# Replacing a score-maximum pass by a norm bound, and a DMA half-swap by a permutation matmul, in an attention and mixture-of-experts kernel

## The reference

```python
# x: (8, 2048, 1024); 8 heads of 128
x = x + attn(layernorm(x))
x = x + ffn(layernorm(x))

def attn(x):
    q, k, v = x @ w_aq, x @ w_ak, x @ w_av      # per head, 128 wide
    q, k = rope(q), rope(k)
    # rope: even, odd = split(x, 2)  (the two halves of the 128)
    #       concat([even*cos - odd*sin, even*sin + odd*cos])
    s = q @ k.T / 128 - 1e30 * (i < j)
    return (softmax(s) @ v) @ w_ao

def ffn(x):   # 8 experts, top 2, and a shared expert of the same size
    cw = softmax(top2(x @ router_w.T)), scattered to 8 columns
    y  = sum_e cw[:, e] * ((silu(x @ w1[e]) * (x @ w3[e])) @ w2[e])
    return y + (silu(x @ sw1) * (x @ sw3)) @ sw2
```

## Time and profile before

| | us |
|---|---|
| two runs | 5095.28 and 5520.56 (median 5307.92) |
| the profiled execution, its own time | 5095.1 |
| its span on the slowest core, number 6 | 5093.6 |
| spans of the eight cores | 5062.8 to 5093.6 |
| TensorE matmul busy | 4199.3 (82%) |
| vector engine busy | 1829.2 (36%) |
| scalar engine busy | 578.0 (11%) |
| Q and K of head 0 start | 266.1 |
| last output slice of head 7 done | 1647.6 |

### The profile page before, as it was taken

The page is one execution under the profiler, slowest core; times in us unless marked ns, Lnnn a source line. Parts: engine busy times, 40 slices in busy tenths (PEclk is TensorE's granted clock), DMA queues, the critical chain, the costliest instruction groups (busy, mean ns, idle before and its releaser), DMA issues.

```text
span 5093.6 us, 49716 instructions; the slowest of 8 cores (5062.8 to 5093.6 us)
## 1 busy us (share of the span) xinstructions
PE 4199.3 (82%) x16850; PEld 1700.1 (33%) x16850; DVE 1829.2 (36%) x3012; ACT 578.0 (11%) x917; POOL 358.7 (7%) x393
## 2 busy tenths in 40 slices
PE   5355557555656549999999999999999999999998
PEld 2111112111111214444444444444444444444443
DVE  4654454455444543223223232232232222322323
ACT  0002111201222001001011011010010110110100
POOL 0000000000000001101011011011010010110100
PEclk9666667766676769999999999999999899999997
DMA  4010000000000124434344434444344334344422
GB/s 94 0 22 8 13 13 0 13 13 13 1 10 2 13 21 38 38 34 40 36 38 38 38 34 38 37 38 38 34 38 37 32 35 38 34 38 39 41 28 77
DMA packets 490854, 151.46 MB, mean 30 GB/s; under 512 B 475642, under 2 KB 486250, under 8 KB 490610
## 3 DMA queue, kind: packets, MB, share of 16 engines
q0 software_dynamic: 475488, 122.72, 26.5%
q1 hardware_dynamic: 15122, 25.56, 1.6%
HBM read 254.12 MB, written 8.39 MB: 52 GB/s over the span
## 4 chain that ended last, share of the span: by engine, by line
PE 74%; DVE 16%; issue 4%; DMA 4%; ACT 1%; DVEq 1%; SPq 1%; ACTq 0%
PE ps L844 20%; PE ps L857 20%; PE ps L905 20%; DVE m_all L513 4%; DMA s_sb<-s_sb 3%; DVE s_sb L590 2%; PE ps L555 2%; PE ps L560 2%; PE ps L569 2%; PE ps L594 1%; ACT pT L581 1%; PE ps L640 1%; PE ps L442 1%; DVE ps L575 1%; DVE s_sb L475 1%
## 5 line engine op out<-in xcount | busy, mean ns | idle before, releaser
L844 PE MATMUL ps<-xn_sb,w_sb 128*128 128x512 bf16 x4608 | 1074.8, 387 | 3.8 <-DVE s_sb L827 3.8
L857 PE MATMUL ps<-xn_sb,w_sb 128*128 128x512 bf16 x4608 | 1056.1, 383 | 0.0
L905 PE MATMUL ps<-big,w_sb 128*128 128x512 bf16 x4608 | 1007.6, 382 | 25.5 <-DVE big L878 25.5
L873 DVE TENSOR_TENSOR s_sb<-ps,s_sb 128x512 bf16<-128x512 f32 x512 | 354.2, 692 | 1205.4 <-PE ps L857 1178.7
L844 PEld LDWEIGHTS ps<-xn_sb,w_sb 128*128 128x128 bf16 x4608 | 457.6, 99 | 583.3 <-issue 87.1
L905 PEld LDWEIGHTS ps<-big,w_sb 128*128 128x128 bf16 x4608 | 453.7, 98 | 579.4 <-issue 45.0
L864 ACT ACTIVATE s_sb<-ps 128x512 bf16<-128x512 f32 x576 | 343.9, 597 | 2663.6 <-PE ps L844 2632.3
L857 PEld LDWEIGHTS ps<-xn_sb,w_sb 128*128 128x128 bf16 x4608 | 454.3, 99 | 554.5 <-issue 46.7
L208 POOL DMA_DIRECT2D w_sb<-w x360 | 333.9, 932 | 2961.7 <-PE ps L857 1828.3
L913 DVE TENSOR_TENSOR x_sb<-x_sb,ps 128x512 f32<-128x512 f32 x288 | 197.9, 687 | 835.5 <-PE ps L905 811.9
L581 ACT ACTIVATE pT<-ps,negmh 128x512 bf16<-128x512 f32 x320 | 219.8, 687 | 1201.0 <-DVE ps L575 932.4
(11 more groups left out here) (105 smaller groups left out, 1339.7 us busy)
## 6 DMA issues: line engine op xcount, KB each, us to landing
w_sb<-w POOLq DMA_DIRECT2D x288, 256.0 KB, 6.3
w_sb<-w POOLq DMA_DIRECT2D x72, 512.0 KB, 8.7
big<-x SPq DMA_DIRECT2D x4, 2048.0 KB, 14.7
s_sb<-s_sb SPq DMA_DIRECT2D x128, 64.0 KB, 2.0
out<-big SPq DMA_DIRECT2D x4, 2048.0 KB, 6.8
w_sb<-wv POOLq DMA_DIRECT2D x2, 1024.0 KB, 20.8
w_sb<-wq POOLq DMA_DIRECT2D x8, 256.0 KB, 5.5
w_sb<-wk POOLq DMA_DIRECT2D x8, 256.0 KB, 6.6
```

The source lines that it names most:

```text
L844: e.matmul(o, l, r, start=s0, stop=s1),
L857: e.matmul(o, l, r, start=s0, stop=s1),
L873: e.tensor_mul(o, i, c),
L905: e.matmul(o, l, r, start=s0, stop=s1),
```

## The change

Two things are rewritten in the attention stage, and nothing else.

First, the half-swap of the rotation. Q (and then K) is now made in all four slices first, 32 matmuls in a row into `ps0` to `ps3`. After them come four steps, one for each slice: cast to bf16, a matmul by a constant 128x128 matrix of 0, 1 and -1 that swaps and signs the halves (into `ps4` or `ps5`), the product with the cosines, the product of the swapped bank with the sines, and the sum. The two DMAs of each slice are gone.

Second, the constant of the head. Instead of the largest score, a bound on it is used: the largest squared norm of a query times the largest squared norm of a key, root taken by Ln and Exp, times 1.02. The squares are made by the vector engine into `pT`, a buffer for each of Q and K, summed over the partitions by a one-column matmul, and reduced on one partition. `emit_mh` is gone; its spreading matmul now ends `emit_passA`, ahead of the next head's Q and K. The matrix is one more 32 KB constant that is loaded at the start.

```diff
+    P = np.zeros((128, 128), dtype=np.float32)
+    for rr in range(64):
+        P[rr, rr + 64] = -1.0
+        P[rr + 64, rr] = 1.0
+    pmat = np.ascontiguousarray(P.T).astype(ml_dtypes.bfloat16)
...
+    t_pmat = dma(ld, "sync", pmat_sb[:, :], d["c_pmat"])
...
             for ts in range(NTS):
-                sl = ts % 2
-                bank = ps[which * 2 + sl]
+                bank = ps[ts]
                 for kc in range(KC):
...
+            for ts in range(NTS):
+                sl = ts % 2
+                bank = ps[ts]
+                pqb = ps[4 + sl]
                 te = bank_cons(bank, "vector",
                                lambda e, o=qb, i=bank.ap[:, :]: e.tensor_copy(o, i),
-                               waits=[qb_swap_tok[sl]])
+                               waits=[qb_free_tok[sl]])
+                qb_free_tok[sl] = bank_prod(pqb,
+                                            lambda e, o=pqb.ap[:, :], r=qb:
+                                            e.matmul(o, pmat_sb[:, :], r,
+                                                     start=True, stop=True),
+                                            waits=[te, t_pmat])
...
-                dma(sw_rope4[sl], "sync", qsw[0:64, :], qb[64:128, :],
-                    waits=[te, sw_last_t2[sl]])
-                d2 = dma(sw_rope4[sl], "sync", qsw[64:128, :], qb[0:64, :])
-                t2 = b.emit("vector",
-                            lambda e, o=rope_t1[1], i=qsw, c=tsn: e.tensor_mul(o, i, c),
-                            waits=[t_sn, d2], incs=[(dv, 1)])[0]
+                bank_cons(pqb, "vector",
+                          lambda e, o=rope_t1[1], i=pqb.ap[:, :], c=tsn:
+                          e.tensor_mul(o, i, c),
+                          waits=[t_sn])
...
     def emit_passA(h):
-        for qi in range(NTT):
-            for ck in range(qi // 4 + 1):
-                bank = ps[4 + ck % 2]
-                bank_prod(bank,
-                          lambda e, o=bank.ap[:, :],
-                          l=qs[:, qi * 128:(qi + 1) * 128],
-                          r=ks[:, ck * 512:(ck + 1) * 512]:
-                          e.matmul(o, l, r, start=True, stop=True),
-                          waits=[rope_done[h]])
-                bank_cons(bank, "vector",
-                          lambda e, i=bank.ap[:, :], o=m_all[:, ci:ci + 1]:
-                          e.reduce_max(o, i, axis=AX.X))
+        sq_scr = [pT[:, 0:512], pT[:, 512:1024]]
+        for which in range(2):
+            src = qs if which == 0 else ks
+            t_prev_mm = pT_free[0]
+            for ts in range(NTS):
+                tsq = b.emit("vector",
+                             lambda e, o=sq_scr[which],
+                             i=src[:, ts * 512:(ts + 1) * 512]: e.tensor_mul(o, i, i),
+                             waits=[rope_done[h], t_prev_mm], incs=[(dv, 1)])[0]
+                t_prev_mm = bank_prod(bank,
+                                      lambda e, o=bank.ap[0:1, :], r=sq_scr[which],
+                                      s0=(ts == 0), s1=(ts == NTS - 1):
+                                      e.matmul(o, onesb[:, :], r, start=s0, stop=s1),
+                                      waits=[tsq], last=True)
+            bank_cons(bank, "vector",
+                      lambda e, o=mh_row[0:1, which:which + 1], i=bank.ap[0:1, :]:
+                      e.reduce_max(o, i, axis=AX.X))
...
     for h in range(NH):
-        t_macc = emit_passA(h)
+        t_negmh = emit_passA(h)
...
-        t_negmh = emit_mh(h, t_macc)
```

More of the change, by code:

```diff
@@ L107, in host_consts @@
     return {"c_cs": cs_full, "c_sn": sn_signed, "c_mask": maskM,
-            "c_identb": identb, "c_identf": identf}
+            "c_identb": identb, "c_identf": identf, "c_pmat": pmat}
 def build_nc(dbg=False):
@@ L129, in build_nc @@
     d["c_identf"] = nc.dram_tensor("c_identf", [128, 128], F32, kind="ExternalInput").ap()
+    d["c_pmat"] = nc.dram_tensor("c_pmat", [128, 128], BF16, kind="ExternalInput").ap()
     d["out"] = nc.dram_tensor("out", [T, DM], F32, kind="ExternalOutput").ap()
@@ L152, in build_nc @@
     identf = nc.alloc_sbuf_tensor("identf", [128, 128], F32)
+    pmat_sb = nc.alloc_sbuf_tensor("pmat_sb", [128, 128], BF16)
     onesb = nc.alloc_sbuf_tensor("onesb", [128, 1], BF16)
@@ L174, in build_nc @@
     negmh = nc.alloc_sbuf_tensor("negmh", [128, 1], F32)
+    mh_sb = nc.alloc_sbuf_tensor("mh_sb", [1, 8], F32)
     bigf = big[:, :].bitcast(F32)
@@ L235, in build_nc @@
     t_constsg = (ldg, ldg.n)
-    t_identb = t_identf = t_mask = t_eb = t_consts
+    t_identb = t_identf = t_mask = t_eb = t_pmat = t_consts
     t_rw = t_cs = t_sn = t_constsg
@@ L421, in build_nc @@
     rope_qb = [sbf[:, i * 512:(i + 1) * 512] for i in range(2)]
-    rope_sw = [sbf[:, 1024 + i * 512: 1024 + (i + 1) * 512] for i in range(2)]
     rope_t1 = [sf[:, 1024 + i * 512: 1024 + (i + 1) * 512] for i in range(2)]
@@ L425, in build_nc @@
     invl_row = sf[0:1, 2560:3072]
[L426 to L429, removed]
+    mh_row = mh_sb[0:1, 0:8]
+    qb_free_tok = [None] * 2
     qk_free = [None, None]
@@ L469, in emit_qkv_rope @@
                               last=(kc == KC - 1))
+            for ts in range(NTS):
+                sl = ts % 2
+                bank = ps[ts]
+                pqb = ps[4 + sl]
                 qb = rope_qb[sl]
-                qsw = rope_sw[sl]
                 tcs = csn[:, ts * 512:(ts + 1) * 512]
@@ L475, in emit_qkv_rope @@
                                lambda e, o=qb, i=bank.ap[:, :]: e.tensor_copy(o, i),
-                               waits=[qb_swap_tok[sl]])
+                               waits=[qb_free_tok[sl]])
[4 more added lines that the diff above has]
+                                            waits=[te, t_pmat])
                 bank_cons(bank, "vector",
-                          lambda e, o=rope_t1[0], i=bank.ap[:, :], c=tcs: e.tensor_mul(o, i, c),
+                          lambda e, o=rope_t1[0], i=bank.ap[:, :], c=tcs:
+                          e.tensor_mul(o, i, c),
                           waits=[t_cs])
-                dma(sw_rope4[sl], "sync", qsw[0:64, :], qb[64:128, :],
-                    waits=[te, sw_last_t2[sl]])
-                d2 = dma(sw_rope4[sl], "sync", qsw[64:128, :], qb[0:64, :])
-                qb_swap_tok[sl] = d2
-                t2 = b.emit("vector",
-                            lambda e, o=rope_t1[1], i=qsw, c=tsn: e.tensor_mul(o, i, c),
-                            waits=[t_sn, d2], incs=[(dv, 1)])[0]
-                sw_last_t2[sl] = t2
+                bank_cons(pqb, "vector",
+                          lambda e, o=rope_t1[1], i=pqb.ap[:, :], c=tsn:
+                          e.tensor_mul(o, i, c),
+                          waits=[t_sn])
                 b.emit("vector",
@@ L494, in build_nc @@
     rope_done = [None] * NH
-    mh_trans_tok = [None]
+    pT_free = [None]
     def emit_passA(h):
@@ L515, in emit_passA @@
[L515 to L519, removed]
-        bank = ps[6]
[L521 to L530, removed]
+        sq_scr = [pT[:, 0:512], pT[:, 512:1024]]
@@ new lines, in emit_passA @@
+        nb = [ps[6], ps[7]]
+        for which in range(2):
+            src = qs if which == 0 else ks
+            bank = nb[which]
+            t_prev_mm = pT_free[0]
[12 more added lines that the diff above has]
+                      e.reduce_max(o, i, axis=AX.X))
@@ new lines, in emit_passA @@
+        b.emit("vector",
+               lambda e: e.tensor_mul(mh_row[0:1, 2:3], mh_row[0:1, 0:1],
+                                      mh_row[0:1, 1:2]),
+               incs=[(dv, 1)])
+        t_mm2 = b.emit("vector",
+               lambda e: e.tensor_scalar_add(mh_row[0:1, 2:3], mh_row[0:1, 2:3], 1e-30),
+               incs=[(dv, 1)])[0]
+        t_ln = b.emit("scalar",
+                      lambda e: e.activation(mh_row[0:1, 3:4], mh_row[0:1, 2:3], AF.Ln),
+                      waits=[t_mm2], incs=[(ac, 1)])[0]
@@ L531, in emit_mh @@
+        t_bd = b.emit("scalar",
+                      lambda e: e.activation(mh_row[0:1, 2:3], mh_row[0:1, 3:4], AF.Exp,
+                                             scale=0.5),
+                      incs=[(ac, 1)])[0]
+        tneg = b.emit("vector",
+                      lambda e: e.tensor_scalar_mul(mh_row[0:1, 3:4], mh_row[0:1, 2:3],
+                                                    -1.02 / DH),
+                      waits=[t_bd], incs=[(dv, 1)])[0]
+        bank = ps[6]
         bank_prod(bank, lambda e, o=bank.ap[:, 0:1]:
-                  e.matmul(o, ones1[:, :], mh_row[0:1, 1:2], start=True, stop=True),
+                  e.matmul(o, ones1[:, :], mh_row[0:1, 3:4], start=True, stop=True),
@@ L603, in emit_passB @@
         qk_free[par] = (pe, pe.n)
+        pT_free[0] = (pe, pe.n)
     emit_v(0)
```

2 lines of the change are left out of this document (removed).

## The result

The changed kernel takes 0.946 of the time of the kernel before, with a 95% interval of 0.9422 to 0.9499: faster, as forecast. The forecast of 4835 us against the 5095.1 us of the profiled execution is a ratio of 0.949. The plain median of its 13 runs is 4902.25 us.

A forecast was written before the change was run, and what follows sets the result against it. The attention part was taken as bound by the vector engine's steps and DMA waits. Gains of 187.7 us (first pass) and 72.9 us (Q, K and rotation) off 5095.1 us gave 4835 us, range 4780 to 4900.

The forecast's parts named there:

- The first pass: Last scaled output to first Q matmul: 14.4 us instead of 37.3 in heads 1 to 6; 187.7 us gained over all heads.
- Q, K and rotation: First Q matmul to next mask: 40.3 us a head instead of a mean of 48.7; 72.9 us gained in all.
- Head 0: Its Q, K and rotation stretch, after dense V matmuls: 37.9 us instead of 49.6, a gain of 11.7.
- The second pass: Attention work after the mask, 82.2 us in head 1: keeps its instructions and its length.
- The sum: Whole kernel: gains of 187.7 and 72.9 us make 260.6, taken from 5095.1 us.
- core 6's slow stretch: Feed-forward window where core 6 was granted 0.83 of the clock against core 5's 1.00; 26 us, kept in the forecast.
- The lower end, 4780: Lower end of the range: both blocks fast in a third of the heads, and core 6 without its 26 us.
- The rotation without gain: Both blocks of 32 matmuls stay at 1.2 GHz, so seven heads gain nothing in Q and K; 4900 us, chance 0.12.
- table loads: Ln and Exp need different tables, two loads of 1.28 us a head, 20.5 us in all; 4855 us, chance 0.03.
- The reduced clock in the feed-forward stage: Less idle time beforehand prolongs slow-clock stretches in the dense stage; about 5320 us if throughout, chance 0.03.

The follow-up runs named there:

- the work in the lulls: Changed kernel with five unused matmuls behind each of the first three swap matmuls of a block; one execution, spans 4780 to 4785 us, no ratio formed.
- The norm bound alone: Changed kernel with the old DMA half-swap and two banks for Q and K; ratio 0.9558 to the kernel before, spans 4856 to 4862 us.
- the swap matmul alone: Kernel before with the new blocks of 32 and swap matmul, old score-maximum pass and constant kept; ratio 0.9828, spans 4995 to 5002 us.

## Why the prediction was right, point by point

- **The first pass** was put at 14.4 us and takes 14.3 in the six heads whose pass is followed by Q, with a step of 1.33 as worked out. The choice that decided, a matmul released at the lower clock's 0.76, was right: from 442.87 to 443.63 it takes 0.76, and the granted clock of the pass is 0.50. Head 7's pass, with the old constant behind it, was to gain 26.5 and gained 26.6 (from last output to mask 41.7 before and 15.1 now).
- **Q, K and rotation** were put at 40.3 us and have a mean of 39.3 in six heads and 36.8 in head 4 (37.9 put). The 9.8 from the first swap matmul to the next block are 9.7. The blocks were put at 9.4 each; Q blocks take 8.9 to 9.6 and K blocks 8.1 to 8.5 in most heads. So the K blocks were mis-sized by about 1 us. They follow shorter lulls, of 2.6 us between swaps, and reach the fast pace sooner than the Q blocks do after the sparse first pass. That the lulls set it is shown by the work in the lulls; why these lulls cost 1 us less than the pass is not.
- **Head 0** was put at 37.9 and takes 37.8 (52.1 from its first Q matmul to head 1's, less 14.3).
- **The second pass** is 82.0 to 82.8 us against 81.6 to 83.1: unchanged, as costed.
- **The sum.** From the first Q matmul to the last output core 6 took 1381.5 us (266.1 to 1647.6) and takes 1116.4 (269.0 to 1385.4). That is 265.1 less; 260.6 were forecast. The seven windows of the rotation, the K blocks in the main, came out some 7 us shorter than put. The V matmuls of heads 4 to 7 (30.3 us instead of 28.5) and the eight second passes (660 us in all instead of 658) take nearly 4 of that back, which leaves the total nearer to the forecast than its terms are. The 4835 us also keep core 6's slow stretch, 26 us; without it the forecast is 4808, and the cores took 4802.
- **A bound with a slip.** The lower end, 4780, does not follow from its terms: two fast blocks in a third of the heads are 13 us and the stretch is 26, so it should be near 4796. Nothing hangs on it.
- **A booking error that cancelled.** The windows to the mask held the old constant's 2 us, which I gave to the rotation. The norm bound alone showed it. The total was not touched, since both parts were in the change: luck, as far as the two terms go.
- **The rivals.** The rotation without gain is refuted by the swap matmul alone, table loads by the one load in the trace. The reduced clock in the feed-forward stage does occur, in both kernels. The runs of the result have it more often in the changed one, 8 of 13 against 3 of 10, too few to tell. Why it comes, and whether a faster attention part brings it on, was not tested, so this rival stays open.

## What to carry to other kernels

When a DMA in a chain is replaced by a matmul, look at what stands ahead of that matmul in TensorE's queue. Here 32 products did, and with the swap moved next to its slice the same instructions were worth another 80 us. A chain of small hand-overs costs its latencies and not its work: exchange the loops so that two chains run beside each other, or put its links where an engine waits anyway, and check that no link lands ahead of work that is ready.

The times say nothing on how tight the norm bound is. With `w_aq` all zeros every score is 0, and so is the bound but for the 1e-30 under its root. With other weights a bound far above the true scores would make all exponentials of a row small, and no run here shows how far that can go.

## What the hardware showed that I had not expected

Extra matmuls made the kernel faster. Fifteen unused ones in each block's lulls raised the granted clock of the stretch from 0.72 to 0.95. They shortened the 32 products of the K block, with the swap ahead of them, from 8.5 us or more to 7.1.

I had also left open whether a slice's products behind short pauses run at 3.4 or 1.7 us. With a pause of 1.08 us ahead of each swap they took 1.89.
